# The ends of a feed-forward loop: loads and LoRA split reordered in the first passes, the last tile by halves and turned on TensorE

## The reference

```python
# x: (64, 64, 1024); 4096 positions of 1024 features
x = x + attn(einsum('bct,bcd->bdt', x, W[itok]), qkvw, qkvb, ow, ob)
# then, with y = x after attention:
base = y @ W.T
logits = y @ Wr.T                     # 8 experts, plus 5.0 for the language
w = softmax(top2(logits));  h = y @ A.T   # per expert, rank 16
z = base + 2.0 * einsum(h, gates(w), B)   # LoRA
zb = z.astype(bfloat16)
qg, sg = quant(zb * inv_gate);  qu, su = quant(zb * inv_up)   # row max / 127
gate = qg @ w_gate.T * sg * s_gate;  up = qu @ w_up.T * su * s_up
inter = clip(silu(gate) * up, -10, 10).astype(bfloat16)
qi, si = quant(inter * inv_inter)
out = x + qi @ w_down.T * si * s_down
```

## Time and profile before

| What | Value |
|---|---|
| median of 3 runs | 2148.84 us (2146.85 to 2151.29) |
| profiled execution, its own time | 2151.06 us |
| profiled execution, span | 2149.4 us |
| TensorE busy | 2075.9 us, 97% of the span |
| VectorE, GpSimd, ScalarE busy | 65%, 65%, 49% |
| mean granted TensorE clock | 0.994 of full speed |
| the loop starts, about | 1484 us |
| one pass in the middle (linear product of 2064.39 to that of 2084.40) | 20.0 us |
| TensorE busy, 1484 to 1504 us | 16.63 of 20.00 us |
| TensorE busy, 2114.8 to 2149.4 us | 17.92 of 34.60 us, granted clock 0.80 |

### The profile page before, as it was taken

How to read it: one execution, slowest core, us unless ns; L and a number is a source line. 1 busy time by engine, 2 the same in 40 slices (tenths; PEclk the granted TensorE clock), 3 DMA queues, 4 the chain that set the end, 5 groups by cost and what they waited for, 6 DMA issues and landing times.

```text
span 2149.4 us, 45962 instructions
## 1 busy us (share of the span) xinstructions
PE 2075.9 (97%) x18120; PEld 1689.5 (79%) x18120; DVE 1407.1 (65%) x2395; ACT 1045.3 (49%) x1364; POOL 1397.0 (65%) x1138
## 2 busy tenths in 40 slices
PE   6999989999999999899998899999999999999996
PEld 6888878888778878788886788887777787787784
DVE  5354565555565445655457855656788888888887
ACT  4366565665566555656555321223444344344343
POOL 7888888888798898889886700001455555555553
PEclk9999999999999999999999999999999999999998
DMA  3355564555645456455557255468344344434433
GB/s 126 83 111 130 105 145 111 116 124 113 156 93 118 108 113 118 133 117 109 124 114 234 100 197 176 150 187 245 81 108 112 99 101 114 105 94 117 107 78 98
DMA packets 413166, 267.05 MB, mean 124 GB/s; under 512 B 275779, under 2 KB 344515, under 8 KB 412483
## 3 DMA queue, kind: packets, MB, share of 16 engines
q1 hardware_dynamic: 409554, 260.33, 48.1%
q0 software_dynamic: 2864, 3.28, 0.9%
q10 hardware_dynamic: 576, 1.05, 0.1%
HBM read 152.92 MB, written 50.33 MB: 95 GB/s over the span
## 4 chain that ended last, share of the span: by engine, by line
PE 79%; POOL 10%; DMA 5%; DVE 3%; issue 2%; ACT 1%; SPq 0%; POOLq 0%; DVEq 0%; ACTq 0%
PE acc L798 32%; PE acc L1744 16%; PE acc L1212 6%; PE att L1212 6%; PE att L1771 5%; POOL w_slot_lo L397 4%; POOL w_raw L400 3%; PE att L1714 3%; PE acc L1780 2%; PE att L827 2%; POOL w_slot_hi L395 2%; PE acc L1753 2%; DMA w_raw<-wu 2%; PE att L854 2%; DMA x_raw<-x 1%
## 5 line engine op out<-in xcount | busy, mean ns | idle before, releaser
L798 PE MATMUL acc<-y_hi,w_slot_hi 128*128 128x512 f32 x1344 | 532.6, 396 | 13.1 <-issue 7.5
L798 PE MATMUL acc<-y_lo,w_slot_hi 128*128 128x512 f32 x1344 | 524.7, 390 | 0.0
L798 PE MATMUL acc<-y_hi,w_slot_lo 128*128 128x512 f32 x1344 | 524.2, 390 | 0.0
L397 POOL TENSOR_TENSOR w_slot_lo<-w_raw,w_slot_hi 128x512 fp32r<-128x512 f32 x329 | 433.6, 1318 | 26.3
L798 PEld LDWEIGHTS acc<-y_hi,w_slot_hi 128*128 128x128 f32 x1344 | 253.0, 188 | 72.2 <-issue 16.0
L400 POOL TENSOR_TENSOR w_raw<-w_raw 128x512 f32<-128x512 f32 x188 | 252.0, 1340 | 75.9 <-DMA w_raw<-wu 72.2
L798 PEld LDWEIGHTS acc<-y_hi,w_slot_lo 128*128 128x128 f32 x1344 | 252.9, 188 | 53.5
L798 PEld LDWEIGHTS acc<-y_lo,w_slot_hi 128*128 128x128 f32 x1344 | 253.3, 188 | 50.0
L623 DVE TENSOR_REDUCE top<-att 128x8 f32<-128x512 f32 x126 | 86.4, 686 | 250.1 <-PE att L827 242.0
L654 DVE TENSOR_TENSOR unit<-acc,unit 128x512 f32<-128x512 f32 x144 | 99.4, 690 | 223.3 <-PE acc L798 218.4
L395 POOL CAST w_slot_hi<-w_raw 128x512 fp32r<-128x512 f32 x329 | 225.9, 687 | 12.1
(11 more groups left out here) (184 smaller groups left out, 3953.4 us busy)
## 6 DMA issues: line engine op xcount, KB each, us to landing
w_raw<-wu SPq DMA_DIRECT2D x188, 256.0 KB, 3.2
c_raw<-context_T SPq DMA_DIRECT2D x16, 1024.0 KB, 6.2
f_x_all<-x_T SPq DMA_DIRECT2D x32, 512.0 KB, 4.8
f_xr_all<-x_T SPq DMA_DIRECT2D x32, 512.0 KB, 6.1
out<-f_raw SPq DMA_DIRECT2D x31, 512.0 KB, 3.4
context_T<-cx SPq DMA_DIRECT2D x60, 256.0 KB, 3.4
x_raw<-x SPq DMA_DIRECT2D x27, 512.0 KB, 4.6
xa<-xT SPq DMA_DIRECT2D x12, 1024.0 KB, 7.2
```

What stands on the lines that cost most here:

```text
L397: pool.tensor_tensor(w_lo[:, k], raw, w_hi[:, k].bitcast(F32), ALU.subtract).then_inc(w_set, 1)
L798: ins = pe.matmul(bank, w[:, k, c, :], v[:, k, c, :], start=(k in (0, 1, 5) and c == 0 and i == 0), stop=(c == C // 2 - 1 and i == 2), ski ...
```

## The change

Start of the loop: SyncE's queue gets a helper `next_x`. The x tile of pass 2 is loaded first, then the input scales, the x tile of pass 3, and behind it `sg_all`, `su_all`, `ii_all` and `sd_c`; `gate` of pass 3 waits for these instead of `scaled` of pass 2. GpSimd issues the load of `dn_w` in pass 2 instead of pass 1, after the input scales have landed. In pass 1 TensorE turns `hg` before the router product and VectorE splits it before `route`.

End of the loop: in pass 32 TensorE does linear and LoRA for the first 512 columns and then for the second. In pass 33 VectorE and GpSimd scale the last tile by halves, and the row maximum is taken from two half maxima. The codes of the last tile are turned by TensorE into the PSUM banks of z and clamped from there (`turn_last`, `clamp_last`) instead of by DMA. In pass 34 the two silu products stand on VectorE (`gated_last`), and `gate` of the last tile and its sigmoid are issued in pass 33. The last down product reports after each half, and `last_output` scales, adds and releases each half for its store.

ScalarE's operations are put into functions (`sigmoid`, `rounded`, `inner_rounded`, `inner_out`) with the same instructions as before; `gate_up` becomes `gate_or_up(t, i, has)`, called for i = 0 and 1.

```diff
--- before.py
+++ after.py
...
-    amax, rinv = (at(n, [P, 3], F32, high + 32 * i) for i, n in enumerate(("amax", "rinv")))
+    amax, rinv = (at(n, [P, w], F32, high + 32 * i) for i, (n, w) in enumerate((("amax", 8), ("rinv", 3))))
...
+    qT_ps = [z_ps[:, i].bitcast(BF16).rearrange("p (c n) -> p c n", n=P) for i in range(2)]
...
+        def next_x(t):
+            sp.wait_ge(a_mm, t)
+            sp.wait_ge(xl_set, t)
+            load(sp, x_sb[(t + 1) % 2], t + 1, x_in[(t + 1) % 2])
+
         outputs_stored(sp)
-        with nc.allow_non_contiguous_dma(reason="1024 scales, once"):
-            sp.dma_start(sd_c[:], s_down.rearrange("(c p) -> p c", p=P)).then_inc(vec_in, 16)
+        next_x(1)
+        sp.wait_ge(w_lo_set, C)
+        load_vector(ig_all, inv_gate, inv_in)
+        load_vector(iu_all, inv_up, inv_in)
+        next_x(2)
         load_vector(sg_all[:], s_gate, vec_in)
         load_vector(su_all[:], s_up, vec_in)
         load_vector(ii_all[:], inv_inter, vec_in)
-        sp.wait_ge(w_lo_set, C)
-        load_vector(ig_all, inv_gate, inv_in)
-        load_vector(iu_all, inv_up, inv_in)
+        with nc.allow_non_contiguous_dma(reason="1024 scales, once"):
+            sp.dma_start(sd_c[:], s_down.rearrange("(c p) -> p c", p=P)).then_inc(vec_in, 16)
 
         for t in range(TILES + 4):
-            if 1 <= t < TILES - 1:
...
+            if 3 <= t < TILES - 1:
+                next_x(t)
...
-            if 2 <= t < TILES + 2:
+            if 2 <= t < TILES + 1:
...
         def body(t, j, has):
-            if isinstance(t, int) and t == 1:
-                outputs_stored(pool)
-                pool.dma_start(dn_w[:], wdT.rearrange("(c p) n -> p c n", p=P)).then_inc(dn_in, 16)
             if has(2):
                 if isinstance(t, int) and t == 2:
+                    outputs_stored(pool)
                     pool.wait_ge(inv_in, 32)
-                pool.wait_ge(zb_set, t * 2 - 2)
+                    pool.dma_start(dn_w[:], wdT.rearrange("(c p) n -> p c n", p=P)).then_inc(dn_in, 16)
                 pool.wait_ge(qb_set, t * 2 - 4)
-                pool.tensor_tensor(xs[1], zb[:], iu_all, ALU.mult).then_inc(xu_set, 1)
-            if has(3):
+                if isinstance(t, int) and t == TILES + 1:
+                    for b in range(2):
+                        cols = slice(b * HALF, (b + 1) * HALF)
+                        pool.wait_ge(zb_set, t * 2 - 3 + b)
+                        pool.tensor_tensor(xs[1][:, cols], zb[:, cols], iu_all[:, cols], ALU.mult).then_inc(xu_set, 1)
+                else:
+                    pool.wait_ge(zb_set, t * 2 - 2)
+                    pool.tensor_tensor(xs[1], zb[:], iu_all, ALU.mult).then_inc(xu_set, 1)
+            if has(3) and not (isinstance(t, int) and t == TILES + 2):
                 pool.wait_ge(sg_set, t - 2)
                 pool.tensor_tensor(silu[:], gt[:], silu[:], ALU.mult).then_inc(p1_set, 1)
                 pool.wait_ge(p1_set, t - 2)
...
         def body(t, j, has):
+            if isinstance(t, int) and t > TILES:
+                if t == TILES + 1:
+                    rounded(t, 0)
+                    sigmoid(t)
+                    rounded(t, 1)
+                    sigmoid(t + 1)
+                if t < TILES + 3:
+                    inner_rounded(t)
+                    inner_out(t)
+                return
             if has(3):
-                act.wait_ge(gt_set, t - 2)
-                act.wait_ge(ib_set, t - 3)
-                act.activation(silu[:], gt[:], ACT.Sigmoid).then_inc(sg_set, 1)
+                sigmoid(t)
...
-                dve.wait_ge(vec_in, 64)
                 dve.wait_ge(inv_in, 32)
...
         def gate(t, j):
+            if isinstance(t, int) and t == 3:
+                dve.wait_ge(vec_in, 64)
             dve.wait_ge(gu_mm, t * 2 - 5)
...
         def inner(t, j):
-            dve.wait_ge(p2_set, t - 2)
+            if not (isinstance(t, int) and t == TILES + 2):
+                dve.wait_ge(p2_set, t - 2)
             dve.wait_ge(xi_set, t - 3)
...
+        def scaled_half(t, b):
+
+            cols = slice(b * HALF, (b + 1) * HALF)
+            dve.wait_ge(zb_set, t * 2 - 3 + b)
+            dve.wait_ge(qb_set, t * 2 - 4)
+            dve.tensor_tensor(xs[0][:, cols], zb[:, cols], ig_all[:, cols], ALU.mult).then_inc(xg_set, 1)
+
+        def half_max(i, b):
+            dve.wait_ge((xg_set, xu_set)[i], TILES + b)
+            dve.tensor_reduce(amax[:, 4 + 2 * i + b:5 + 2 * i + b], xs[i][:, b * HALF:(b + 1) * HALF], AX.X, ALU.max,
+                              apply_absolute_value=True).then_inc(m8_set, 1)
+
+        def scale_halves(t, j, i):
+            dve.wait_ge(m8_set, TILES + 3 + i)
+            row_max(i, amax[:, 4 + 2 * i:6 + 2 * i], amax_set)
+            scale(i, (j + 2) % 4, amax_set, sc_set, rinv_set, t * 2 - 3 + i)
+
+        def clamp_last(i):
+            dve.wait_ge(a_mm, TILES + i + 1)
+            dve.tensor_scalar(qT[i][:], qT_ps[i], QMAX, -QMAX, ALU.min, ALU.max).then_inc(qT_set, 1)
+
+        def gated_last(t, j):
+
+            dve.wait_ge(sg_set, t - 2)
+            dve.wait_ge(gt_set, t - 2)
+            dve.tensor_tensor(silu[:], gt[:], silu[:], ALU.mult).then_inc(xg_set, 1)
+            up(t, j)
+            dve.wait_ge(xg_set, TILES + 2)
+            dve.wait_ge(ut_set, t - 2)
+            dve.tensor_tensor(silu[:], silu[:], ut[:], ALU.mult).then_inc(xg_set, 1)
+            dve.wait_ge(xg_set, TILES + 3)
+
+        def last_output(t, j):
+
+            dve.wait_ge(si_mm, t - 3)
+            dve.tensor_copy(si_sb[:], si_ps).then_inc(si_set, 1)
+            dve.wait_ge(si_set, t - 3)
+            dve.wait_ge(o_out[j % 2], pair_count(t - 6, j))
+            dve.wait_ge(xr_in[j % 2], pair_count(t - 4, j))
+            for b in range(2):
+                half = slice(b * C // 2, (b + 1) * C // 2)
+                dve.wait_ge(d_mm, t - 3 + b)
+                dve.tensor_tensor(o_sb[j % 2][:, half], d_ps[:, b].rearrange("p (c n) -> p c n", n=P),
+                                  si_sb[:].unsqueeze(1).broadcast_to([P, C // 2, P]), ALU.mult).then_inc(o1_set, 1)
+                dve.wait_ge(o1_set, t - 3 + b)
+                for c in range(b * C // 2, (b + 1) * C // 2):
+                    ins = dve.scalar_tensor_tensor(o_sb[j % 2][:, c], o_sb[j % 2][:, c], sd_c[:, c:c + 1],
+                                                   xr[j % 2][:, c], ALU.mult, ALU.add)
+                ins.then_inc(o2_set, 1)
+
         def body(t, j, has):
             if isinstance(t, int) and t == TILES + 1:
-                for piece in (scaled, gate, scale_gate, scale_up, up, output, inner):
-                    piece(t, j)
-                clamp(t, 0)
+                scaled_half(t, 0)
+                half_max(0, 0)
+                half_max(1, 0)
+                scaled_half(t, 1)
+                half_max(0, 1)
+                scale_halves(t, j, 0)
+                half_max(1, 1)
+                scale_halves(t, j, 1)
+                gate(t, j)
+                up(t, j)
+                clamp_last(0)
+                output(t, j)
+                clamp_last(1)
+                inner(t, j)
+                gate(t + 1, j + 1)
                 inner_scale(t, j)
-                clamp(t, 1)
+                diagonal(t, j)
                 output_scale(t, j)
-                diagonal(t, j)
                 return
             if isinstance(t, int) and t == TILES + 2:
-                for piece in (gate, up, inner, inner_scale, output, diagonal, output_scale):
+                gated_last(t, j)
+                inner(t, j)
+                for piece in (inner_scale, diagonal, output, output_scale):
                     piece(t, j)
                 return
             if isinstance(t, int) and t == TILES + 3:
-                output(t, j)
-                dve.wait_ge(xr_in[j % 2], pair_count(t - 4, j))
-                for c in range(C):
-                    ins = dve.scalar_tensor_tensor(o_sb[j % 2][:, c], o_sb[j % 2][:, c], sd_c[:, c:c + 1],
-                                                   xr[j % 2][:, c], ALU.mult, ALU.add)
-                    if c in (C // 2 - 1, C - 1):
-                        ins.then_inc(o2_set, 1)
+                last_output(t, j)
                 return
             if has(2):
                 scaled(t, j)
@@ -1680,12 +1773,14 @@
...
+            if isinstance(t, int) and t == 1:
+                lora(t, j)
             if has(0):
                 route(t, j)
             if has(3):
...
-            if has(1):
+            if has(1) and not (isinstance(t, int) and t == 1):
...
-        def linear(t, j, first):
+        def linear(t, j, first, bs=(0, 1)):
...
-            for b in range(2):
+            for b in bs:
...
+        def turn_last(t, i):
+
+            pe.wait_ge(qb_set, t * 2 - 3 + i)
+            for c in range(C):
+                ins = pe.transpose(qT_ps[i][:, c], qb[i][:, c * P:(c + 1) * P], ident_b[:])
+            ins.then_inc(a_mm, 1)
+
...
```

(70 more changed lines are left out.)

7 lines of the change are left out of this document (1 added, 6 removed).

## The result

The changed kernel is slower: 2183.86 us (median of 6 runs, 2179.33 to 2190.6) beside 2147.89 us for the kernel before (6 runs, 2146.77 to 2153.36), a ratio of 1.0158 with a 95% interval of 1.0141 to 1.0175. The prediction said 2143.9 us, with a range of 2141.2 to 2147.2. The profiled execution has a span of 2183.5 us (own time 2185.13 us), 34.1 more than before, at a mean granted clock of 0.993.

The account below looks back on a forecast made before the run. TensorE was taken to bound the loop, with holes only at its two ends. Gains of 3.6 (start), 0.2 and 1.05 (end) sum to 4.9 us, giving 2143.9 us from the median; range 2141.2 to 2147.2.

Parts of the forecast that it names:

- TensorE sets the pace of the loop, nothing that the change does to another engine there can show: Middle of the loop, 1545 to 2112 us: TensorE is the bound, so its gain at the start is kept.
- rival 4: Pass 3's gate waits for late vectors and s_down; kernel slower, 2155 us if they land at 1528; chance 0.04.
- The start: Passes 1 and 2: no TensorE hole before router(2), at 1500.7 against 1504.32; 3.6 us gained.
- Rivals 3: Start's gain eaten because pass 2's transposes land 3 us later than their cover: 2146.9 us; chance 0.08.
- The end: Last tile, passes 32 to 34: 0.2 us gained up to clipping of tile 31, then 1.05 after its last rounding.
- In pass 33 a half-wide VectorE product that lasts over 1 us: Last tile's scaling by halves: a sign that VectorE is stretched beside GpSimd; no stretch would mean the prediction is wrong.
- The first clamp from PSUM: Last tile's turned codes: starts near 2121.5 in the old frame, takes 0.8, the middle of bounds 0.42 and 1.23.
- rival 1: The end gives nothing: clamps of 1.23 and a fall of TensorE's clock leave only the start, 2145.4 us; chance 0.25.
- The second silu product: Tile 31 on VectorE: stretched past 1.5 us beside GpSimd's add, ending at 2134.2 in the old frame.
- The last rounding: Tile 31: ends at 2137.64 in the old frame, 3.24 after clipping starts, with 0.2 us gained by clipping's start.
- +8.1: Last output: the final VectorE column operation ends 8.1 us after the last rounding.
- +10.7: Last output: span ends 10.7 us after the last rounding, store and landing included, against 11.76 before; 1.05 gained.

Follow-up runs that it names:

- e2: Kernel before with only GpSimd's two waits exchanged (qb, then zb): 2187.32 us, ratio 1.0157 to the kernel before.
- e1: Changed kernel with GpSimd's old order of waits (zb, then qb) put back in the loop: 2144.54 us, ratio 0.9963 to the kernel before.
- e5: Kernel before with the changes at the end alone, GpSimd's waits in their old order in the loop: 2148.03 us, ratio 0.9985.
- e6: Changed kernel with GpSimd's loop product waiting for VectorE's product instead of zb and qb: 2144.34 us, ratio 0.9967 to the kernel before.
- e3: Changed kernel with VectorE's two waits of `scaled` exchanged too, so zb comes last: 2178.28 us, ratio 1.0109 to the kernel before.
- e7: Changed kernel with one more, always met wait on GpSimd's loop product: 2186.5 us, ratio 1.0172 to the kernel before.
- e4: Kernel before with the changes at the start alone, GpSimd's waits in their old order: 2145.52 us, ratio 0.9965.
- e8: Kernel before with GpSimd's two waits exchanged in one of four loop bodies (passes 4, 8, 12, ...): 2187.17 us, ratio 1.0179.

## Why the prediction was wrong

**The step that failed** is "TensorE sets the pace of the loop, nothing that the change does to another engine there can show". It rested on a list of waits in which TensorE waits for nobody, and such a list does not say how much room there is. VectorE had 2 us in a pass of 20, and the order of two starts 40 ns apart decided whether it needed them: in the changed kernel the loop took 21.3 us a pass instead of 20.0, 39.1 us in all. The prediction had the mechanism in hand: it took from the earlier trace rows that VectorE and GpSimd take turns, that 3.12 stands against 1.23, and that VectorE came first at 2115.45 against 2115.49. It used this for the last tile alone. The exchanged lines are in the diff, and no cost was worked out for them; nor was there a rival that had the loop itself slower (the slower kernel of rival 4 came from a late load in pass 3). e2 shows that these lines alone cost 1.57%, e1 that without them the same change gains 0.37%. The Trainium skill, page "SBUF — State Buffer", section "SBUF: two separate sides", states it as a rule for such a pair (VectorE with two inputs in SBUF, GpSimd reading SBUF): whichever of the two engines starts first has the shared ports for its whole instruction, and the other one is blocked. The rows agree with it (1.22 and 3.19, or 2.13 and 3.15). What the runs add is that the loser can stay the loser.

**The start** was right: 3.56 us gained (forecast 3.6), router(2) without a wait ahead of it, nothing eaten in pass 2 or 3. Rivals 3 and 4 did not come: the second clamp of pass 2 ended at 1515.6 (0.7 of it the later start of this stage), and the gate of pass 3 found its vectors landed.

**The end** was right in its mechanisms and too small in its size, 2.14 for 1.25. Rows of VectorE, kernel after, pass 33 on (to compare with the old frame, take off 36.24):

```profile
2151.69 0.69 DVE L1691 TENSOR_TENSOR f_raw<-f_zb,f_raw 128x512 f32<-128x512 bf16 x1 [0.82 <-ACT f_zb L1527]
...
2157.26 0.69 DVE L1705 TENSOR_SCALAR f_qT<-acc 128x1024 bf16<-128x1024 bf16 x1 [1.10 <-PE acc L1862]
...
2160.47 0.69 DVE L1705 TENSOR_SCALAR f_qT<-acc 128x1024 bf16<-128x1024 bf16 x1 [1.06 <-PE acc L1862]
...
2164.95 1.22 DVE L1660 TENSOR_TENSOR f_raw<-f_raw,f_sd_c 128x1024 f32<-128x1024 f32 x1
...
2167.54 1.99 DVE L1715 TENSOR_TENSOR f_silu<-f_silu,f_ut 128x512 f32<-128x512 f32 x1
...
2172.38 0.43 DVE L1639 TENSOR_SCALAR f_xi<-f_xi 128x512 f32<-128x512 f32 x1
...
2179.78 1.14 DVE L1732 SCALAR_TENSOR_TENSOR f_raw<-f_raw,f_sd_c,f_xr_all 128x128 f32<-128x128 f32 x4
```

- "In pass 33 a half-wide VectorE product that lasts over 1 us": not here (0.68 and 0.69; in the second half VectorE had the turn and GpSimd took 1.67). That was one of the prediction's own signs of being wrong. But it came in e5, e1 and e6 (the second half, 1.66, 1.67 and 1.45), the kernels whose loop runs at 20.0 us a pass, as the prediction had assumed. From the four transposes to the end it is 33.1 us in those three, and 32.6 with the turn (here and in e3); e7, with the slow loop, has 1.04 and 33.1.
- The first clamp from PSUM starts at 2157.26, which is 2121.02 in the old frame; forecast 2121.5. It takes 0.69. So rival 1's clamp of 1.23 did not come, and the middle of 0.8 was too high. The estimate of 0.66 from the cycle table of the Trainium skill's page "VectorE: DVE Perf Modes" was nearer. The rule of its section "Why PSUM operands drop a tier", a 2x mode at most for 16-bit operands in PSUM, agrees with the run.
- TensorE's eight transposes take 0.61 in all, beside the 0.5 used. Their row:

```profile
2156.61 0.61 PE L1862 MATMUL acc<-f_ident_b,f_qb 128*128 128x128 bf16 x8
```

- The second silu product is stretched to 1.99 beside GpSimd's add, as forecast ("past 1.5 us").
- The last rounding ends at 2172.81, 2136.57 in the old frame: 1.07 gained where 0.2 was forecast. That is the term of the sum that was mis-sized. By the rows above, 0.5 of the missing 0.9 was there when the first clamp began (2121.02 for 2121.5), 0.6 at the second's end (2124.92 for 2125.5), 0.8 at the end of output_scale (2129.93 for 2130.7) and 0.9 at the end of the second silu product (2133.29 for 2134.2). The reciprocal came 1 us early (ScalarE starts at 2153.71, 2117.47 in the old frame, forecast 2118.45), but half of that was lost, because TensorE was at the down product and output_scale until 2156.6 and turned the codes, complete at 2156.0, only then.
- From there "+8.1" to the last column operation (2180.92) and "+10.7" to the end (2183.5) came out to the tenth.

Start and end together are 5.7 us, 0.27%; with the 33.1 us end of e1 and e6 they are 5.2, 0.24%. e1's interval (0.18% to 0.55%) holds both, and the 0.23% forecast too. e4 and e5 do not separate well: e4 gains 0.35%, e5 0.15%, and e1, which has both, 0.37%, all with intervals of 0.15 to 0.19 to either side.

## What to carry to other kernels

Where VectorE and GpSimd are released by the same event, and both then read two operands from SBUF, look at who starts first and by how much. If it is some tens of ns, as here, the place of one register instruction can decide it: tie the second to the first by a semaphore (e6), which cost nothing here. And before an engine is called out of the way, compare its slack in a pass (here 2 us) with the longest hold-up that another engine can give it (here 1.9 us for the lost turn, and 1.9 again on the diagonal of the next pass). A reordering of "waits that are both needed anyway" belongs in the sum like any other edit.

## What the runs showed of the hardware

- One register instruction on GpSimd behind the wait that is met last costs 0.08 to 0.1 us between the release and the instruction after it (0.16 to 0.18 against some 0.08); a wait itself, added alone, changes nothing that the time shows (e7).
- The loop has two steady courses, 20.0 and 21.3 us a pass, and e3 shows both in one execution. A single lost turn leads from the first to the second, and no trace shows a way back (e3, e8); before the residual adds begin, a lost turn heals itself (pass 3 of e4, and of e3).
- A diagonal of 128 columns, 0.28 us of work, stands 2.15 us behind a GpSimd product of 1024 columns that started 0.2 us before it.
- A clamp of 1024 bf16 columns from PSUM takes 0.69 us on VectorE; from SBUF it took 0.42.
